# Attention and mixture-of-experts block on one core: rows of y laid out by token and read in 4 KB runs, VectorE's last stage in another order with a second buffer for the shared expert's gated rows

## The reference

```python
y = y.at[tok].add(swiglu(xg, W1[e], W2[e], W3[e]) * w[:, None])   # over 32 experts, 4 per token
z = swiglu(xf, Ws1, Ws2, Ws3)                                     # shared expert
out = x + y + z
```

## Time and profile before

| | us |
|---|---|
| median of 3 runs | 887.0 |
| lowest and highest of the 3 | 878.15 and 888.27 |
| profiled execution, its own time | 876.93 |
| span of the profiled execution | 875.2 |
| what lies around the span (876.93 - 875.2) | 1.73 |

### The profile page before, as it was taken

How to read it: one execution, slowest core, us unless ns; L and a number is a source line. 1 busy time by engine, 2 the same in 40 slices (tenths; PEclk the granted TensorE clock), 3 DMA queues, 4 the chain that set the end, 5 groups by cost and what they waited for, 6 DMA issues and landing times.

```text
span 875.2 us, 17144 instructions
## 1 busy us (share of the span) xinstructions
PE 766.0 (88%) x3710; PEld 577.9 (66%) x3711; DVE 519.2 (59%) x1496; ACT 447.4 (51%) x1834; POOL 376.6 (43%) x352
## 2 busy tenths in 40 slices
PE   7776999999898998989867769989999998999770
PEld 5554677767576776667645448777787887886440
DVE  1773227777869494959585525545555554553678
ACT  2454777676666767666713004554555554554000
POOL 1001232338383837465573604555555564654000
PEclk9988999999999999999996989999999999999995
DMA  6345322335253534399358876665765564554996
GB/s 243 97 134 158 115 85 84 110 102 199 98 175 109 184 129 169 124 347 363 123 181 312 304 248 215 197 221 178 224 195 167 177 185 143 181 180 132 350 361 211
DMA packets 132865, 164.29 MB, mean 188 GB/s; under 512 B 11253, under 2 KB 120771, under 8 KB 132803
## 3 DMA queue, kind: packets, MB, share of 16 engines
q1 hardware_dynamic: 118979, 121.66, 44.1%
q0 software_dynamic: 13824, 41.96, 13.3%
HBM read 84.77 MB, written 78.81 MB: 187 GB/s over the span
## 4 chain that ended last, share of the span: by engine, by line
PE 55%; DVE 22%; DMA 7%; ACT 7%; issue 6%; SPq 2%; DVEq 1%; ACTq 0%; POOLq 0%
PE psum L1481 14%; PE psum L1256 9%; PE psum L1336 9%; PE psum L1378 7%; PE psum L1493 7%; PE psum L1420 4%; ACT sm L788 3%; DVE big L1234 3%; DMA xblk<-expert_lists 3%; DVE ln1g L946 3%; PE psum L1431 3%; DMA big<-in_x 2%; DVE x L983 2%; PE psum L1399 2%; PE psum L1279 1%
## 5 line engine op out<-in xcount | busy, mean ns | idle before, releaser
L679 POOL DMA_INDIRECT y_d<-sm,yrow x160 | 154.8, 968 | 143.9 <-issue 89.7
L1481 PE MATMUL psum<-big,xbT 128*128 x640 | 168.1, 386 | 1.0 <-DVE xbT L1206 0.4
L788 ACT ACTIVATE sm<-psum,nmax 128x77 f32<-128x77 f32 x512 | 157.3, 365 | 16.0 <-DVE nmax L1096 16.0
L1378 PE MATMUL psum<-big,pT 128*128 (+1 forms) x640 | 148.4, 388 | 2.1 <-DVE res L1111 2.1
L665 POOL DMA_INDIRECT expert_lists<-rows,slot x128 | 125.6, 982 | 51.0 <-issue 38.5
L1336 PE MATMUL psum<-big,xnT 128*128 (+2 forms) x384 | 140.3, 515 | 3.6 <-ACT sm L788 3.0
L646 POOL TENSOR_TENSOR sm<-sm,sinv 128x1232 f32<-128x1232 f32 x32 | 72.1, 2253 | 160.4 <-DVE sinv L1120 160.2
L1378 PEld LDWEIGHTS psum<-big,pT 128*128 128x128 f32 x640 | 122.6, 196 | 18.4 <-DVE res L1111 2.2
L788 ACT ACTIVATION_READ_ACCUMULATOR sm<-psum,nmax 128x1 f32 x512 | 127.2, 248 | 0.0
L1481 PEld LDWEIGHTS psum<-big,xbT 128*128 128x128 f32 x640 | 110.4, 193 | 12.5 <-issue 3.8
L1336 PEld LDWEIGHTS psum<-big,xnT 128*128 128x128 f32 x384 | 70.9, 191 | 60.7 <-issue 52.1
(11 more groups left out here) (183 smaller groups left out, 1020.5 us busy)
## 6 DMA issues: line engine op xcount, KB each, us to landing
xblk<-expert_lists SPq DMA_DIRECT2D x160, 160.0 KB, 2.3
y_d<-zero SPq DMA_DIRECT2D x32, 512.0 KB, 4.0
big<-y_d SPq DMA_DIRECT2D x32, 512.0 KB, 8.6
big<-in_L_ffn_W SPq DMA_DIRECT2D x16, 320.0 KB, 7.8
expert_lists<-filler SPq DMA_DIRECT2D x32, 160.0 KB, 2.7
xin<-in_x SPq DMA_DIRECT2D x36, 128.0 KB, 2.1
big<-in_x SPq DMA_DIRECT2D x8, 512.0 KB, 3.5
xres<-in_x SPq DMA_DIRECT2D x8, 512.0 KB, 5.1
```

The lines of the kernel that those rows point to most:

```text
L679: pool.indirect_dma_start(out=y_d, out_offset=bass.IndirectOffsetOnAxis(ap=yrow[:, q:q + 1], axis=0), in_=eo[:, q, :], in_offset=None).the ...
L788: last = nc.scalar.activation(sm[:, t % 2, h * SK:(h + 1) * SK], head_scores(h, h + 1), ACT.Exp, bias=nmax[:, t % 2, h:h + 1], accum_out=s ...
L1378: last = mm(o_ps[:, 0:D], pT[:, to % 2, c, :], VO[:, bass.ds(batch(jo, po), 1), c, :], start=c == 0, stop=c == CK - 1)
L1481: last = mm(bank(2 + q % 2)[:, 0:2 * H], xbT[:, q % 2, k, :], ew[:, bass.ds(e, 1), k * 2 * H:(k + 1) * 2 * H], start=k == 0, stop=k == KC - 1)
```

## The change

Two things are changed together.

- **The y rows.** Choice k of a token now has row 4 * token + k. The iota and the step of `pair` change their constants. `load_y` now issues one DMA for each tile t of a group, of the same 512 KB: in it every partition takes one run of 4 KB, its token's four rows. The `ysum` slot is laid out (t, k, d) in place of (k, t, d), so each operand of `sum_group` from it is four runs of 256 elements, 1024 elements apart, and not one run of 1024. The number of DMAs, bytes and operations stays.
- **VectorE's end.** `sh_end` gets a second buffer (a part of the tile `early`), picked by g % 2, and a gate of groups 5 to 7 waits for `z_psum` (g - 1) * 2, which is `s_down(g - 2)`. The order of the gates, sums and adds is written out. TensorE's, ScalarE's and SP's orders stay.

```diff
-        ysum = big[:, 0:final_at].rearrange("p (i k t d) -> p i k t d", i=RING, k=TOPK, t=TG)
+        ysum = big[:, 0:final_at].rearrange("p (i t k d) -> p i t k d", i=RING, t=TG)
...
-        sh_end = big[:, gate_at + KC * GT:gate_at + 2 * KC * GT].rearrange("p (k n) -> p k n", k=KC)
+        sh_end = [x.rearrange("p (k n) -> p k n", k=KC)
+                  for x in (big[:, gate_at + KC * GT:gate_at + 2 * KC * GT], early[:, 1, :, :].rearrange(as_k))]
...
-                for k in range(TOPK):
-                    sp.dma_start(ysum[:, g % RING, k, :, :], y_d[g * GT + k * T:(g + 1) * GT + k * T, :]
-                                 .rearrange("(t p) d -> p t d", p=P)).then_inc(ld_y[g % RING], 16)
+                for t in range(TG):
+                    at = (g * GT + t * P) * TOPK
+                    sp.dma_start(ysum[:, g % RING, t, :, :], y_d[at:at + P * TOPK, :]
+                                 .rearrange("(p k) d -> p k d", k=TOPK)).then_inc(ld_y[g % RING], 16)
...
-                   pool.iota(pair[:, :, :], [[P, TG], [T, TOPK]], base=0, channel_multiplier=1, **kw),
+                   pool.iota(pair[:, :, :], [[P * TOPK, TG], [1, TOPK]], base=0, channel_multiplier=TOPK, **kw),
...
-                nc.vector.tensor_scalar(pair[:, :, :], pair[:, :, :], float(GT), None, ALU.add).then_inc(s["pair_ready"], 1)
+                nc.vector.tensor_scalar(pair[:, :, :], pair[:, :, :], float(GT * TOPK), None, ALU.add).then_inc(s["pair_ready"], 1)
...
-                wait(dve, "z_psum", g * 2)
+                wait(dve, "z_psum", (g if g <= MID else g - 1) * 2)
...
-                sg_in, sh_out = (sg, sh) if g < MID else (sg_end, sh_end)
+                sg_in, sh_out = (sg, sh) if g < MID else (sg_end, sh_end[g % 2])
...
-                    out_sb = ysum[:, p, k, :, :] if k < TOPK - 1 else final[:, p, :, :]
-                    so_far = ysum[:, p, k - 1, :, :] if k else base[:, g * TG:(g + 1) * TG, :]
-                    nc.vector.tensor_tensor(out_sb.rearrange(flat), ysum[:, p, k, :, :].rearrange(flat),
-                                            so_far.rearrange(flat), ALU.add).then_inc(s["ysum_step"], 1)
+                    out_sb = ysum[:, p, :, k, :] if k < TOPK - 1 else final[:, p, :, :]
+                    so_far = ysum[:, p, :, k - 1, :] if k else base[:, g * TG:(g + 1) * TG, :]
+                    nc.vector.tensor_tensor(out_sb, ysum[:, p, :, k, :], so_far, ALU.add
+                                            ).then_inc(s["ysum_step"], 1)
...
-            for g in range(MID, NG):
-                shared_gate(g, 0)
-                shared_gate(g, 1)
-                sum_group(g - MID)
-                add_shared(g)
-            for g in range(MID, NG):
-                if g == MID:
-                    dve.wait_ge(s["z_added"], 2 * NG)
-                sum_group(g)
+            shared_gate(MID, 0)
+            shared_gate(MID, 1)
+            shared_gate(MID + 1, 0)
+            sum_group(0)
+            add_shared(MID)
+            shared_gate(MID + 1, 1)
+            sum_group(1)
+            shared_gate(MID + 2, 0)
+            add_shared(MID + 1)
+            sum_group(2)
+            shared_gate(MID + 2, 1)
+            shared_gate(MID + 3, 0)
+            sum_group(3)
+            add_shared(MID + 2)
+            shared_gate(MID + 3, 1)
+            assert NG == 2 * MID == MID + 4
+            for g in range(MID, NG):
+                wait(dve, "z_added", 2 * (g + 1))
+                sum_group(g)
+                if g == MID:
+                    add_shared(NG - 1)
...
-                hT = sh if g < MID else sh_end
+                hT = sh if g < MID else sh_end[g % 2]
```

More of the change, by code:

```diff
@@ L227, in attention_moe_kernel @@
         assert gate_at + 2 * KC * GT <= E * EW
-        ysum = big[:, 0:final_at].rearrange("p (i k t d) -> p i k t d", i=RING, k=TOPK, t=TG)
+        ysum = big[:, 0:final_at].rearrange("p (i t k d) -> p i t k d", i=RING, k=TOPK, t=TG)
         final = big[:, final_at:gate_at].rearrange("p (i t d) -> p i t d", i=RING, t=TG)
         sg_end = big[:, gate_at:gate_at + KC * GT].rearrange("p (k n) -> p k n", k=KC)
-        sh_end = big[:, gate_at + KC * GT:gate_at + 2 * KC * GT].rearrange("p (k n) -> p k n", k=KC)
+        sh_end = [x.rearrange("p (k n) -> p k n", k=KC)
+                  for x in (big[:, gate_at + KC * GT:gate_at + 2 * KC * GT], early[:, 1, :, :].rearrange(as_k))]
         xg_mid += [xg[:, 0, :, :], xg[:, 1, :, :]]
@@ L1224, in sum_group @@
                 p = g % RING
-                wait(dve, ld_y[p], (g // RING + 1) * 16 * TOPK)
-                flat = "p t d -> p (t d)"
+                wait(dve, ld_y[p], (g // RING + 1) * 16 * TG)
                 for k in range(TOPK):
```

## The result

| | before | after |
|---|---|---|
| median us (4 runs each) | 884.75 | 871.37 |
| lowest and highest | 878.15 and 888.27 | 869.53 and 873.05 |
| profiled execution, span | 875.2 | 871.3 |
| first y load issued | 805.2 | 810.86 |
| from there to the first sum | 9.66 | 8.44 |

The ratio of the times is 0.9898, with a 95% interval of 0.9853 to 0.9942. The change makes the kernel about 1% faster: clear of no change by its interval, and inside the 2% of the forecast's middle case. The forecast was a ratio of 867.5/876.93 = 0.9893.

The account below looks back on a forecast made before the run. VectorE was taken to bound the end stage, DMA second. VectorE's stretch 8.7 us and first landing 0.7 gave 9.4: 876.93 to 867.5, or 887.0 to 877.6 against the median; range 868 to 882, 68% for 876.5 to 879.5.

Parts of the forecast that it names:

- the forecast's middle case: Whole kernel: time within 2% of the kernel before, given 88%.
- The sum: End stage: 8.7 us from VectorE's stretch and 0.7 from an earlier first sum, together 9.4 us saved.
- the last scatter lands later than 805: Sign of being wrong, at the last scatter into `y_d` before the end stage: landing after 805 us.
- VectorE's stretch: End stage from first sum's start to last sum's end: 47.2 us work plus 1.0 waiting, 48.2 in place of 56.9.
- First landing: Start of the end stage: group 0 of y lands earlier with 4 KB runs, first sum starts 0.7 us earlier.
- The DMA rate: y loads in the end stage: 410 GB/s with 4 KB runs, bounds 353 and 426; stores at 353.
- the DMA rival: End stage: y still comes at 353 GB/s and DMA is the bound, gain 5.9 us, 881.1; chance 15%.
- Strided sums: VectorE's sums on runs of 256: 0 extra time; rival with 1.55 times the time, 899 us, chance 3%.
- The broadcast row: Profile row for sums: 128x1024 operation with broadcast operands, runs of 32, 1226 ns against 1225 flat; taken as nearest case.
- the reduction: Profile row for sums: innermost step not one element, 1063 ns against 686, factor 1.55; taken as upper bound.
- The clock: TensorE before down(6): rival that 1.9 us idle lowers the clock, down(6) 1.9 us longer, gain 7.5, 879.5; chance 10%.
- The scatter to other addresses: Scatter of y rows beside the block loop: 0 cost, only its last 2.43 us piece exposed; half as slow again costs 1.2.

Follow-up runs that it names:

- the order alone: Kernel before with only the new order and the second buffer, y rows, loads and sums kept in 1 KB runs: ratio 0.9929, end stretch 63.2 us.
- one buffer: Changed kernel with one buffer for the gated rows, so each gate waits for down(g-1) again: ratio 0.9918, end stretch 64.0 us.
- the late gate: Changed kernel with gate (5,0) behind sum(0) and not ahead of it: ratio 0.9922, end stretch 63.8 us.
- the later last gate: Changed kernel with gate (7,1) behind sum(4) and the last add ahead of sum(7): ratio 0.9888, end stretch 59.7 us.
- the run with both: Changed kernel with group 5's sum on GpSimd and gate (7,1) behind sum(4): ratio 0.9919, end stretch 62.5 us.

## Why the prediction was right, point by point

**The sum.** A gain of 9.4 us was forecast in the end stage; the end stretch is shorter by 9.6, and the ratio 0.9898 stands beside 0.9893. The absolute 877.6 was set against the median of three runs, 887.0; with a fourth that median is 884.75, and 884.75 - 9.4 = 875.4 is to be compared with 871.37. Those 4 us are as much as the ratio's interval leaves open (0.0044 of 885 us on each side), so no term of the sum can be read from them. That 9.4 and 9.6 lie so close is partly luck: two terms missed in opposite directions (below).

**The signs in the profile.** For an execution like the profiled one the forecast was 867.5, with the first sum near 814.2 and the last sum's end near 862.3. The profiled one after took 873.05 us, with 819.30 and 867.85: 5.1 to 5.6 us later, because the whole end stretch began 5.7 us later. So the sign "the last scatter lands later than 805" came, though it was set too tight, since before the last scatter had landed at 805.11 (802.68 + 2.43). The other two signs of being wrong stayed away, an operation of a sum over 1.3 us and a wait for `big<-y_d` behind the first group. The limit of 1.2 us for VectorE's waits was passed by 0.1.

**VectorE's stretch.** 48.2 us forecast, 48.55 measured, so 8.3 us were saved here where 8.7 was said. The order of events was as listed. The wait at gate(7,1) is 1.30 us in place of 1.0: from the start of down(6) at 838.37 to the SiLU's start at 845.62 it took 7.25 us, where two pieces of 3.45 had been counted.

**First landing.** 0.7 us was the forecast for the earlier first sum. The first profile after gives 1.2, the second the same; this covers what VectorE's stretch lacks. Over all profiles it is 8.4 to 9.7 us from first load to first sum with 4 KB runs (mean of nine 8.9) and 9.0 to 9.8 with 1 KB (mean of five 9.5), so about 0.55. The step was right in the mean, and one profile can miss it by its own size.

**The DMA rate.** 410 GB/s was taken for y; 406 to 413 is what the stage moved between 820 and 840, its stores included. The packet rule of the Trainium skill ("DMA: Bandwidth & Descriptors", section "Why small descriptors are slow (HBM only)") had given an estimated 377. The trace disagrees with that number and agrees with the two 4 KB stretches of the kernel before. The 358 GB/s for a core that the DMA rival took from the Trainium skill ("HBM Reference", section "Specifications (TRN2)") did not bind this core, which ran alone.

**DMA as the next bound.** Forecast for 353 GB/s: a wait of 2.5 us for the last group and a gain of 5.9. The kernel with the order alone shows 1.86 us and 6.8. The mechanism was right, the size 0.9 too pessimistic.

**Strided sums.** 0 forecast, 0 measured: 1225 ns. The broadcast row was the right neighbour, the reduction was not.

**The clock.** The new idle before down(6) is 1.63 us (1.9 forecast), and the clock stayed. The rival was real all the same: with the old order, one buffer, the late gate and the later last gate TensorE was idle for 3.5 to 5.1 us, and the matmuls behind that took 5.07 to 5.41 us.

**What was missed.** The scatter to other addresses was put at 0, with 1.2 us as the worst, because only its last piece is exposed. In the profiles the loop itself is longer with the new addresses, which that argument had no place for. Either the term is not quite 0 or the loop's length in profiles is no measure of it; see above.

## What to carry to other kernels

When one engine feeds another and also has long work of its own, put the short piece that releases the other engine first, even ahead of data that has already been asked for; here that, with the second buffer, removed 6.8 of 70 us, and a faster transfer alone removed 0.5. Then ask what is the next bound: on top of the order the transfer was worth 2.8 us. And price an idle engine before giving it work: GpSimd and VectorE adding side by side took longer than VectorE alone.

## What the runs showed of the hardware

- GpSimd beside VectorE: with GpSimd adding 128x1024 float32 operands at the same time, VectorE's same operation went from 1.225 us to 3.05 and more, and both ran at about one operation in 3.25 us. A gate of 128x512 with one operand in PSUM took its usual 0.68 us beside GpSimd's additions (the run with both).
- The end stage moved 404 to 415 GB/s in stretches of 10 us with loads in 4 KB runs (820 to 860, after) and 348 to 364 with loads in 1 KB runs (820 to 860, before), its 1 KB stores included and with the same bytes in each DMA. SP issued the first 16 loads, from first to last start, in 8.2 us with 4 KB runs (after) and in 18.6 with 1 KB (before).
- TensorE's granted clock: behind idle times of 1.5 to 1.6 us in the end stage it stayed at 2.4 GHz (column 1.00), behind 3.5 to 5.1 us it was at 1.2 GHz for a few us (0.50), at a cost of 1.5 to 1.8 us on matmuls that otherwise take 3.60 to 3.72. In the run with both, down(7) came behind 9.10 us of idle and took 6.46.
